# Seven copied row pairs in six buffers, gathers that wait for the rows in front, a written-out first pair and a deep block in the last pair, in an xDeepFM kernel on one NeuronCore

## The chip, the core and the metric

The kernel runs on one NeuronCore of a Trainium2 chip. The metric is device time in microseconds (us). The kernel before takes 447.75 us, the median of 3 runs (447.04 to 449.23).

## What is computed

The reference is one forward pass of xDeepFM over a batch of 512, with 26 features of a 32-wide embedding (`M`, `E`) and 13 dense inputs. Cut to its core:

```python
emb = tables[feat_idx, sparse]                       # (512, 26, 32)
linear_out = lin_sparse_w[feat_idx, sparse].sum(-1) + dense @ lin_dense_w
x0 = xk = emb
for w, bb in ((conv1_w, conv1_b), (conv2_w, conv2_b)):    # 128 outputs each
    hp = einsum('bhd,bmd->bhmd', xk, x0).reshape(-1, h * 26, 32)
    xn = sigmoid(einsum('oi,bid->bod', w, hp) + bb)
    xk = xn[:, :64]                                  # goes on to the next layer
    res.append(xn[:, 64:])                           # goes to the output
cin_out = concat(res).sum(-1) @ cin_w + cin_b
h1 = tanh(concat(emb, dense) @ W1 + b1)              # 845 -> 1024
h2 = tanh(h1 @ W2 + b2); h3 = tanh(h2 @ W3 + b3)     # 512, 256
return linear_out + cin_out + h3 @ deep_w + deep_b + bias
```

## The kernel before, in words

The 512 samples are worked through in 16 **pairs** (`NPAIR`), each of two chunks `c` of 16 samples; a chunk has 16 x 32 = 512 columns, so a tile of a pair has 1024. Five engines run programs of their own and meet through counters (semaphores).

**Rows in.** GpSimd's `gather(i)` fetches the embedding rows of pair `i` with 7 indirect DMAs (line 348). SyncE's queue writes them to HBM in another layout (`lay_out`, tensor `laid`), then reads them back in two forms: `fetch(i)` brings a raw tile of 26 rows (`raw`), and `copy(n)` brings a row pair broadcast to 128 partitions (`copied`, 2 DMAs of 256 KB). SyncE's queue also loads the deep weights (`load_piece`). It works strictly in order: per pair `NC` copies, a `lay_out` after the fourth, the `fetch` at the end. A copy into a buffer waits until TensorE has finished the tile that used it last (`main_done`).

**Layer 1.** ScalarE casts raw to `x` (`x_high`, line 524), VectorE computes the low part (`x_low`, line 629). TensorE forms sums of feature pairs (`sums_of`, line 396, three a pair), ScalarE squares them (`squares`), TensorE contracts the squares (`layer1`, line 412, two a pair), and ScalarE's `sigmoid` (line 544) gives `xk`.

**Layer 2.** It has 13 tiles `t` a pair (`T2`). For a tile, VectorE multiplies `xk` by rows of `x0` spread over the partitions (the product, line 696), and TensorE contracts the product (`main`, line 434). The spread rows come in one of two ways: for the tiles in `COPIED` from the buffers that DMA fills, for the tiles in `SPREAD` from PSUM, where TensorE puts them with a selection matmul (`spread_tile`, line 424). Sums and spreads share three PSUM slots (`ring`); an entry waits until the entry three places ahead of it in the list that `enter` makes has been read. Products of spread tiles go through three buffers (`prod`).

**The order** on TensorE is written out by tables: a pair has four groups (`GROUPS`), and `SUMS_IN`, `SPREADS_IN`, `L1_IN` say what stands in front of or behind the mains of each group. Before pair 0, TensorE runs `WARM` matmuls (line 447) whose result nothing uses.

**The deep part** comes last: ScalarE and GpSimd split the transposed embeddings into `xt_hi` and `xt_lo` (line 369), GpSimd splits ten weight pieces, and TensorE runs 8 + 4 + 2 blocks of `D1`, `D2`, `D3` outputs (line 491); a block of the first layer is 21 matmuls.

## Time and profile before

| | |
|---|---|
| median of 3 runs | 447.75 us |
| the profiled execution | 447.28 us, of which the span is 445.5 us |
| mean granted TensorE clock | 0.981 |
| TensorE busy | 423.0 us, 95% |
| VectorE busy | 318.5 us, 71% |
| ScalarE, GpSimd busy | 161.1 us, 164.2 us |
| DMA | 64.03 MB, mean 144 GB/s |
| chain that ended last | TensorE 74%, VectorE 11%, issue 11% |

Pair 0 begins when the first sums are formed and ends with its `main` of tile 12 at 69.24 us; pairs 1 to 14 follow without a visible seam up to 354.21 us, then pair 15 up to about 372 us, and the deep part up to 443.9 us. Busy shares are means over these stages. Ends of matmuls are modelled, so the distance between the starts of two rows tells more than the length of one. A row of the timeline with "x4" merges four records; an fp32 matmul leaves two records.

### The profile page before, as it was taken

Reading aid. Unit: us, or ns where it says so; the run is one execution under the profiler, and the core shown is the slowest. Engines: PE = TensorE matmul, PEld = TensorE weight load, DVE = VectorE, ACT = ScalarE, POOL = GpSimd, SP = SyncE. Lnnn points to the kernel's source line nnn. Section 1 sums busy time; section 2 is a strip of 40 time slices with the busy share of each in tenths; the row PEclk is TensorE's granted clock in tenths of the full one; section 3 lists DMA queues with packets and bytes.
Section 4 is the critical chain, followed back from the end, with each engine's and each line's share of the span. In section 5 each row is a group of like instructions: output and inputs, shape, how many; then the busy total and the mean of one; then the engine's idle time right before and its main releaser. Section 6 shows DMA issues by size and latency. Waiting matters only on the chain.

```text
span 445.5 us, 5390 instructions
## 1 busy us (share of the span) xinstructions
PE 423.0 (95%) x1961; PEld 176.5 (40%) x1961; DVE 318.5 (71%) x356; ACT 161.1 (36%) x264; POOL 164.2 (37%) x146
## 2 busy tenths in 40 slices
PE   3687989999999999999999999999999989999997
PEld 3662322333233332323333333323333225887784
DVE  3104568898989898988989898989889794522121
ACT  3027224444352634444453526344443321111011
POOL 6734516243343516172434436060000096840000
PEclk9978789999999999999999999999999999999999
DMA  5445477787878686877877686949657631310000
GB/s 189 91 113 119 100 181 168 186 198 171 184 187 194 171 205 162 192 181 175 196 176 190 179 195 157 227 125 211 183 148 162 146 94 47 97 48 1 0 0 0
DMA packets 38304, 64.03 MB, mean 144 GB/s; under 512 B 19601, under 2 KB 22033, under 8 KB 38278
## 3 DMA queue, kind: packets, MB, share of 16 engines
q1 hardware_dynamic: 34694, 61.93, 54.7%
q0 software_dynamic: 3584, 1.76, 4.2%
q8 instruction: 15, 0.25, 0.2%
q14 instruction: 11, 0.09, 0.1%
HBM read 61.96 MB, written 1.71 MB: 143 GB/s over the span
## 4 chain that ended last, share of the span: by engine, by line
PE 74%; DVE 11%; issue 11%; ACT 2%; SPq 1%; DVEq 0%; another core or an unknown queue 0%; DMA 0%; ACTq 0%
PE conv L434 32%; PE conv L412 18%; PE conv L491 7%; PE ring L491 7%; DVE copied L696 7%; PE ring L424 5%; PE ring L396 3%; DVE prod L696 3%; ACT sq L573 1%; ACT xk L544 0%; ACT sq L533 0%; DVEq L694 0%; PE conv L510 0%; PE conv L506 0%
## 5 line engine op out<-in xcount | busy, mean ns | idle before, releaser
L348 POOL DMA_INDIRECT emb<-in_table,rows x112 | 128.3, 1146 | 168.8 <-DMA laid<-emb 137.1
L696 DVE TENSOR_TENSOR prod<-ring,xk 128x1024 f32<-128x1024 f32 x112 | 133.8, 1218 | 38.0 <-PE ring L424 29.1
L696 DVE TENSOR_TENSOR copied<-copied,xk 128x1024 f32<-128x1024 f32 x96 | 114.2, 1230 | 0.4
L434 PE MATMUL conv<-prod,w_sb 128*64 128x512 f32 x448 | 114.4, 614 | 0.1
L434 PE MATMUL conv<-copied,w_sb 128*64 128x512 f32 x384 | 96.3, 603 | 2.9 <-DVE copied L696 2.0
L412 PE MATMUL conv<-sq,w_sb 117*64 117x512 f32 x384 | 90.4, 606 | 0.3 <-issue 0.3
L544 ACT ACTIVATE xk<-conv,const_sb 64x512 f32<-64x512 f32 x64 | 43.7, 682 | 126.3 <-PE conv L412 113.1
L533 ACT ACTIVATE sq<-ring 117x512 f32<-117x512 f32 x90 | 48.5, 595 | 31.5 <-PE ring L396 19.5
L434 PEld LDWEIGHTS conv<-copied,w_sb 128*64 128x64 f32 x384 | 24.7, 137 | 67.3 <-issue 38.3
L412 PEld LDWEIGHTS conv<-sq,w_sb 117*64 117x64 f32 x384 | 27.8, 139 | 55.9 <-issue 55.7
L434 PEld LDWEIGHTS conv<-prod,w_sb 128*64 128x64 f32 x448 | 26.7, 137 | 51.3 <-issue 43.4
L629 DVE TENSOR_TENSOR x<-raw,x 26x512 fp32r<-26x512 f32 x32 | 21.8, 683 | 27.7 <-issue 16.0
L424 PE MATMUL ring<-x,sel_sb 58*128 58x512 f32 x224 | 40.1, 418 | 0.4 <-DVE prod L696 0.2
L369 POOL TENSOR_TENSOR xt_lo<-xt,xt_hi 128x512 fp32r<-128x512 f32 (+1 forms) x7 | 14.2, 2061 | 56.4 <-ACT xt_hi L605 56.4
L424 PEld LDWEIGHTS ring<-x,sel_sb 58*128 58x128 f32 x224 | 20.0, 187 | 21.4 <-issue 17.2
L396 PE MATMUL ring<-x,sel_sb 58*117 58x512 f32 x96 | 23.9, 485 | 4.4 <-DVE prod L696 2.4
L724 DVE CAST h_hi<-hf 128x512 fp32r<-128x512 f32 x8 | 6.5, 819 | 26.6 <-ACT hf L617 26.6
L396 PEld LDWEIGHTS ring<-x,sel_sb 58*117 58x117 f32 x96 | 8.7, 173 | 40.6 <-issue 35.1
L546 ACT ACTIVATE res<-conv,const_sb 64x512 f32<-64x512 f32 x32 | 21.9, 684 | 0.8
L447 PE MATMUL conv<-sel_sb 128*117 128x234 f32 x113 | 17.2, 315 | 4.9 <-issue 4.9
L524 ACT ACTIVATE x<-raw 96x512 fp32r<-96x512 f32 x16 | 10.1, 631 | 27.2 <-DMA raw<-laid 25.8
L447 PEld LDWEIGHTS conv<-sel_sb 128*117 128x117 f32 x113 | 16.1, 223 | 6.2 <-issue 6.1
(76 smaller groups left out, 292.2 us busy)
## 6 DMA issues: line engine op xcount, KB each, us to landing
copied<-laid SPq DMA_DIRECT2D x192, 256.0 KB
wpiece<-in_mlp SPq DMA_DIRECT2D x22, 256.0 KB
emb<-in_table,rows POOLq DMA_INDIRECT x112
raw<-laid SPq DMA_DIRECT2D x32, 52.0 KB
laid<-emb SPq DMA_DIRECT2D x16, 96.0 KB, 2.9
sel_f<-in_sel SPq DMA_DIRECT2D x1, 832.0 KB, 5.6
const_sb<-in_const SPq DMA_DIRECT2D x1, 626.0 KB, 4.1
w_sb<-in_w SPq DMA_DIRECT2D x1, 416.0 KB, 6.2
```

The costliest lines, as they stand in the source:

```text
L348: pool.indirect_dma_start(out=emb[0:n, i, j, :], out_offset=None, in_=table, in_offset=bass.IndirectOffsetOnAxis(ap=rows[0:n, i, j:j + 1], ...
L396: mm = nc.tensor.matmul(sums_bank(i, u)[0:UK, c, :], sel1_sb[at:at + XK, u, :], x[i % RX][at:at + XK, :], start=True, stop=True)
L412: mm = nc.tensor.matmul(l1_bank(i, c)[o, :], w1_sb[:, u, o], sq[i % 2][0:UK, u, c, :], start=(u == 0), stop=(u == UT - 1))
L424: mm = nc.tensor.matmul(spread_bank(r)[:, c, :], sel2_sb[at:at + XK, t, :], x[i % RX][at:at + XK, :], start=True, stop=True)
L434: mm = nc.tensor.matmul(conv[i % 2][c * HALF:(c + 1) * HALF, :], w2_sb[:, t, :], prod_of(r)[:, c, :], start=(t == 0), stop=(t == T2 - 1))
L447: nc.tensor.matmul(conv[1][0:UK, 0:2 * UK], sel1_sb[:, 0, :], sel1_sb[:, 0:2, :].rearrange("p u k -> p (u k)"), start=True, stop=True)
L491: mm = nc.tensor.matmul(MLP_BANKS[n % 2], w[0:r, k, mt * P:(mt + 1) * P], h[0:r, k, :], start=(k == 0 and j == 0), stop=(k == kt - 1 and j ...
L533: nc.scalar.activation(sq[i % 2][0:UK, u, c, :], sums_bank(i, u)[0:UK, c, :], ACT.Square)\
L544: nc.scalar.activation(xk[i % 2][q * HALF:(q + 1) * HALF, c, :], bank[0:HALF, :], ACT.Sigmoid, bias=small_sb[0:HALF, C_CB1:C_CB1 + 1]).the ...
L546: nc.scalar.activation(res1[i % 2][c * HALF:(c + 1) * HALF, :], bank[HALF:P, :], ACT.Sigmoid, bias=small_sb[HALF:P, C_CB1:C_CB1 + 1]).then ...
L629: nc.vector.tensor_tensor(x[i % RX][at + XLO:at + XK, :], raw[i % RX][at:at + M, :], x[i % RX][at:at + M, :].bitcast(F32), ALU.subtract).t ...
L696: nc.vector.tensor_tensor(prod_of(r)[:, :, :].rearrange("p c n -> p (c n)"), left[:, :, :].rearrange("p c n -> p (c n)"), xk[i % 2][:, :, ...
```

## The change

Seven tiles instead of six are copied, and six instead of seven spread; the copies go through six buffers (`RC`) instead of five. The spreads of tiles 0 and 1 of a pair stand in the pair before. `gather(i)` waits for the rows of pair `i-1` to land, no longer for their rewritten form in `laid`; pair 1 waited for nothing before and now waits for the rows of pair 0. TensorE's order for pair 0 is written out, with all work of pair 0 and the matmuls for pair 1 in its own sequence. The 113 small warm matmuls become 13 fp32 matmuls of 512 columns on another tensor, which wait for `sel_in`. ScalarE casts `x` of pair 1 after the second sigmoid of pair 0, and VectorE computes the low part of pair 1 after tile 1. The first block of the deep part's first layer is issued in the last pair after tile 7, and waits for the `xt_lo` pieces one by one. Scratch tensors are merged (`lin_row` over `xt`, `clamped` into `wrap`).

```diff
@@ -38,19 +38,18 @@
 GSEM = 4
 RING = 3
 RP = 3
-COPIED = (1, 2, 3, 6, 7, 10)
+COPIED = (2, 3, 5, 6, 7, 10, 11)
 SPREAD = tuple(t for t in range(T2) if t not in COPIED)
 NC, NS = len(COPIED), len(SPREAD)
-RC = 5
+RC = 6
 LAY_AT = 3
+DEEP_AT = 1
 GROUPS = ((0, 1, 2, 3), (4, 5, 6, 7), (8, 9, 10, 11), (12,))
-SPREADS_IN = (((0, 4), (0, 5)), ((0, 8), (0, 9)), ((0, 11), (0, 12)), ((1, 0),))
-SUMS_IN = ({0: ((1, 0), (1, 1), (1, 2)), 2: ((2, 0),), 3: ((2, 1),)},
-           {0: ((1, 2),), 2: ((2, 0),), 3: ((2, 1),)})
-L1_AHEAD = ({0: 0}, {})
-L1_IN = ({0: 1}, {0: 0, 1: 1})
+SPREADS_IN = (((0, 4),), ((0, 8), (0, 9)), ((0, 12), (1, 0)), ((1, 1),))
+SUMS_IN = {0: ((1, 2),), 2: ((2, 0),), 3: ((2, 1),)}
+L1_IN = {0: 0, 1: 1}
 X_LOW_AT, TURN_AT, FOLD1_AT, PIECE_AT = (10, 5), 9, (5, 7), 11
-WARM = 113
+WARM = 13
 
 C_B1, C_B2, C_B3, C_DEEP, C_CB1, C_CB2, C_CIN1, C_CIN2, C_AUX, C_END = 0, 8, 12, 14, 16, 17, 18, 20, 22, 23
 SMALL_AT = 0
...
@@ -240,8 +239,16 @@
 
         for u in range(UT):
             enter(("sums", 0, u))
-        enter(("spread", 0))
-        for i in range(NPAIR):
+        enter(("spread", SPREAD[0]))
+        enter(("spread", SPREAD[1]))
+        for u in range(UT):
+            enter(("sums", 1, u))
+        for r in SPREAD[2:]:
+            enter(("spread", r))
+        for k in range(2):
+            enter(("sums", 2, k))
+            enter(("spread", T2 + SPREAD[k]))
+        for i in range(1, NPAIR):
             for g in range(len(GROUPS)):
                 for j, u in sums_in(i, g):
...
@@ -341,8 +348,8 @@
 
                 if i >= GSEM:
                     pool.wait_ge(rows_in[i % GSEM], ROWS * (i // GSEM))
-                if i >= 2:
-                    pool.wait_ge(laid_in[(i - 1) % RX], LAID * ((i - 1) // RX + 1))
+                if i:
+                    pool.wait_ge(rows_in[(i - 1) % GSEM], ROWS * ((i - 1) // GSEM + 1))
                 for j in range(GJ):
                     n = P if j < NG else ML * PB
                     pool.indirect_dma_start(
@@ -416,7 +423,7 @@
             def spread_tile(r):
 
                 i, t = r // T2, r % T2
-                if t == 0:
+                if t == SPREAD[0]:
                     pe.wait_ge(x_lo_done, 2 * (i + 1))
                 slot_free("spread", r)
...
@@ -435,6 +442,28 @@
                                           start=(t == 0), stop=(t == T2 - 1))
                 mm.then_inc(main_done, 1)
 
+            deep_layers = ((m1_hi, m1_lo, K1, xt_hi, xt_lo), (m2_hi, m2_lo, K2, h1_hi, h1_lo),
+                           (m3_hi, m3_lo, K3, h2_hi, h2_lo))
+
+            def deep(layer, mt):
+
+                hi, lo, kt, xh, xl = deep_layers[layer]
+                start = sum(MT[:layer])
+                n = start + mt
+                if n >= 2:
+                    pe.wait_ge(tanh_done, n - 1)
+                for k in range(kt):
+                    if n == 0:
+                        pe.wait_ge(xt_lo_done, k + 1)
+                    if layer and mt == 0:
+                        pe.wait_ge(h_lo_done, start - kt + k + 1)
+                    r = K1_LAST if layer == 0 and k == K1 - 1 else P
+                    for j, (w, h) in enumerate(((hi, xh), (lo, xh), (hi, xl))):
+                        mm = nc.tensor.matmul(MLP_BANKS[n % 2], w[0:r, k, mt * P:(mt + 1) * P],
+                                              h[0:r, k, :], start=(k == 0 and j == 0),
+                                              stop=(k == kt - 1 and j == 2))
+                mm.then_inc(mlp_done, 1)
+
             pe.wait_ge(const_in, 16)
             pe.wait_ge(w1_step, 2)
             for u in range(UT):
@@ -442,57 +471,63 @@
                                       start=(u == 0), stop=(u == UT - 1))
             mm.then_inc(fix_done, 1)
 
+            pe.wait_ge(sel_in, 16)
+            for k in range(WARM):
+                nc.tensor.matmul(conv[1][:, :], sel2_f[:, 0, :], sel2_f[:, 0:4, :].rearrange("p t o -> p (t o)"),
+                                 start=True, stop=True)
             pe.wait_ge(sel_done, 1)
-            for k in range(WARM):
-                nc.tensor.matmul(conv[1][0:UK, 0:2 * UK], sel1_sb[:, 0, :], sel1_sb[:, 0:2, :].rearrange("p u k -> p (u k)"),
-                                 start=True, stop=True)
             for u in range(UT):
                 sums_of(0, u)
             pe.wait_ge(w1_step, 4)
             layer1(0, 0)
             pe.wait_ge(sel_done, 2)
-            spread_tile(0)
+            spread_tile(SPREAD[0])
+            spread_tile(SPREAD[1])
             layer1(0, 1)
             pe.wait_ge(w2_in, 16)
-            for i in range(NPAIR):
+            for u in range(UT):
+                sums_of(1, u)
+                main(u)
+            spread_tile(SPREAD[2])
+            main(3)
+            spread_tile(SPREAD[3])
+            layer1(1, 0)
+            for r in SPREAD[4:-1]:
+                spread_tile(r)
+            for t in range(4, 8):
+                main(t)
+            spread_tile(SPREAD[-1])
+            layer1(1, 1)
+            for t in range(8, T2 - 1):
+                main(t)
+            for k in range(2):
+                sums_of(2, k)
+                spread_tile(T2 + SPREAD[k])
+            main(T2 - 1)
+            for i in range(1, NPAIR):
                 for g, tiles_now in enumerate(GROUPS):
                     for j, u in sums_in(i, g):
                         sums_of(j, u)
                     for r in spreads_in(i, g):
                         spread_tile(r)
-                    if g in L1_AHEAD[min(i, 1)]:
-                        layer1(i + 1, L1_AHEAD[min(i, 1)][g])
                     for t in tiles_now:
                         main(T2 * i + t)
-                    if g in L1_IN[min(i, 1)] and i + 1 < NPAIR:
-                        layer1(i + 1, L1_IN[min(i, 1)][g])
+                    if i == NPAIR - 1 and g == DEEP_AT:
+                        pe.wait_ge(piece_lo, KW)
+                        pe.wait_ge(l2_read, NPAIR - 1)
+                        deep(0, 0)
+                    if g in L1_IN and i + 1 < NPAIR:
+                        layer1(i + 1, L1_IN[g])
 
             pe.wait_ge(lin_step, 1)
             nc.tensor.matmul(ring[1][0:NPAIR, 1, 0:PB], lin[:, :], ind_sb[:, :], start=True, stop=False)
             nc.tensor.matmul(ring[1][0:NPAIR, 1, 0:PB], emb[0:ML * PB, :, NG, E], ind_sb[0:ML * PB, :],
                              start=False, stop=True).then_inc(lin_done, 1)
 
-            pe.wait_ge(xt_lo_done, K1)
-            pe.wait_ge(l2_read, NPAIR - 1)
-            n = 0
-            for layer, (hi, lo, kt, xh, xl) in enumerate((
-                    (m1_hi, m1_lo, K1, xt_hi, xt_lo), (m2_hi, m2_lo, K2, h1_hi, h1_lo),
-                    (m3_hi, m3_lo, K3, h2_hi, h2_lo))):
-                before = sum(MT[:layer])
+            for layer in range(3):
                 pe.wait_ge(piece_lo, (KW, KW + K2, PIECES)[layer])
-                for mt in range(MT[layer]):
-                    if n >= 2:
-                        pe.wait_ge(tanh_done, n - 1)
-                    for k in range(kt):
-                        if layer and mt == 0:
-                            pe.wait_ge(h_lo_done, before - kt + k + 1)
-                        r = K1_LAST if layer == 0 and k == K1 - 1 else P
-                        for j, (w, h) in enumerate(((hi, xh), (lo, xh), (hi, xl))):
-                            mm = nc.tensor.matmul(MLP_BANKS[n % 2], w[0:r, k, mt * P:(mt + 1) * P],
-                                                  h[0:r, k, :], start=(k == 0 and j == 0),
-                                                  stop=(k == kt - 1 and j == 2))
-                    mm.then_inc(mlp_done, 1)
-                    n += 1
+                for mt in range(1 if layer == 0 else 0, MT[layer]):
+                    deep(layer, mt)
                 if layer == 0:
 
                     pe.wait_ge(fold1_done, NPAIR)
@@ -573,8 +608,8 @@
                     nc.scalar.activation(sq[0][0:UK, u, c, :], sums_bank(0, u)[0:UK, c, :], ACT.Square).then_inc(sq_done, 1)
             act.wait_ge(sel_done, 2)
             sigmoid(0, 0)
+            sigmoid(0, 1)
             x_high(1)
-            sigmoid(0, 1)
             for u in range(UT):
                 squares(1, u)
             sigmoid(1, 0)
...
@@ -677,7 +712,6 @@
             dve.wait_ge(w1_step, 3)
             nc.vector.tensor_copy(w1_sb[:, :, :], w1a_sb[:, :, :]).then_inc(w1_step, 1)
             x_low(0)
-            x_low(1)
 
             for i in range(NPAIR):
                 for t in range(T2):
@@ -698,6 +732,8 @@
                                             xk[i % 2][:, :, :].rearrange("p c n -> p (c n)"),
                                             ALU.mult).then_inc(prod_done, 1)
                     k = min(i, 1)
+                    if i == 0 and t == 1:
+                        x_low(1)
                     if t == X_LOW_AT[k] and i + 2 < NPAIR:
                         x_low(i + 2)
                     if t == FOLD1_AT[k]:
```

**TensorE at the start.** First before, then after: from the warm matmuls on (`sel_sb`, `sel_f`) into pair 0; `sq` is read by `layer1`, `x` by sums (117 rows) and spreads (128 rows).

```order
L447 MATMUL conv<-sel_sb 117x234 x113
L396 MATMUL ring<-x_81,sel_sb 117x512 x6
L412 MATMUL conv<-sq_64,w_sb 64x512 x6
L424 MATMUL ring<-x_81,sel_sb 128x512 x2
L412 MATMUL conv<-sq_64,w_sb 64x512 x6
L396 MATMUL ring<-x_82,sel_sb 117x512 x6
L424 MATMUL ring<-x_81,sel_sb 128x512 x4
L412 MATMUL conv<-sq_65,w_sb 64x512 x6
L434 MATMUL conv<-prod_70,w_sb 64x512 x2
```

```order
L476 MATMUL conv<-sel_f 128x512 x13
L403 MATMUL ring<-x_81,sel_sb 117x512 x6
L419 MATMUL conv<-sq_63,w_sb 64x512 x6
L431 MATMUL ring<-x_81,sel_sb 128x512 x4
L419 MATMUL conv<-sq_63,w_sb 64x512 x6
L403 MATMUL ring<-x_82,sel_sb 117x512 x2
L441 MATMUL conv<-prod_69,w_sb 64x512 x2
L403 MATMUL ring<-x_82,sel_sb 117x512 x2
L441 MATMUL conv<-prod_70,w_sb 64x512 x2
```

The sums of pair 1 now alternate with the first mains of pair 0, and layer 1 of pair 1 stands behind them.

**TensorE where one pair passes into the next.** First before, then after: from the sums ahead of tile 12 to the first mains of the next pair (`prod` and `copied` name the two kinds of product).

```order
L396 MATMUL ring<-x_81,sel_sb 117x512 x2
L424 MATMUL ring<-x_83,sel_sb 128x512 x2
L434 MATMUL conv<-prod_71,w_sb 64x512 x2
L396 MATMUL ring<-x_81,sel_sb 117x512 x2
L424 MATMUL ring<-x_83,sel_sb 128x512 x4
L434 MATMUL conv<-prod_72,w_sb 64x512 x2
L434 MATMUL conv<-copied_75,w_sb 64x512 x2
```

```order
L403 MATMUL ring<-x_81,sel_sb 117x512 x2
L431 MATMUL ring<-x_83,sel_sb 128x512 x2
L441 MATMUL conv<-prod_71,w_sb 64x512 x2
L403 MATMUL ring<-x_81,sel_sb 117x512 x2
L431 MATMUL ring<-x_83,sel_sb 128x512 x2
L441 MATMUL conv<-prod_69,w_sb 64x512 x2
L441 MATMUL conv<-prod_70,w_sb 64x512 x2
L441 MATMUL conv<-copied_74,w_sb 64x512 x2
```

The spread behind the first sums was that of the next pair's tile 0 and is now that of its tile 1; behind the second sums stands one spread (tile 4) instead of two.

**TensorE in the last pair.** After the change, behind tile 7 (before, the spread of the next group followed at once): 21 matmuls of the deep part, of which the first three and the last three are shown, then the spread of tile 12.

```order
L441 MATMUL conv<-copied_72,w_sb 64x512 x2
L441 MATMUL conv<-copied_73,w_sb 64x512 x2
L462 MATMUL conv<-xt_hi,m_hi 128x512
L462 MATMUL conv<-xt_hi,m_lo 128x512
L462 MATMUL conv<-xt_lo,m_hi 128x512
...
L462 MATMUL conv<-xt_hi,m_hi 128x512
L462 MATMUL conv<-xt_hi,m_lo 128x512
L462 MATMUL conv<-xt_lo,m_hi 128x512
L431 MATMUL ring<-x_81,sel_sb 128x512 x2
L441 MATMUL conv<-prod_69,w_sb 64x512 x2
L441 MATMUL conv<-prod_70,w_sb 64x512 x2
```

The block moved from behind the last pair to its middle; tiles 8 to 12 stand behind it.

## Rows read from the trace of the kernel before

**Rows 1.** Page, part 1: busy time, share of the span, instructions, by engine.
```profile
PE 423.0 (95%) x1961; PEld 176.5 (40%) x1961; DVE 318.5 (71%) x356; ACT 161.1 (36%) x264; POOL 164.2 (37%) x146
```

**Rows 2.** Stretches: length, busy PE, PEld, DVE, ACT, POOL (x count), clock, DMA, GB/s.
```profile
42.05:69.24 27.19, 25.74 (x96) 8.00 (x96) 17.05 (x18) 9.36 (x17) 12.18 (x11) 0.81 0.54 133
69.24:354.21 284.97, 284.17 (x1342) 89.99 (x1340) 257.73 (x279) 124.36 (x205) 95.04 (x81) 1.00 0.75 180
354.21:372.10 17.89, 15.49 (x66) 3.72 (x64) 17.07 (x18) 4.44 (x8) 14.17 (x7) 1.00 0.26 75
...
301.00:322.00 21.00, 20.94 (x102) 6.73 (x101) 19.10 (x22) 9.62 (x16) 0.00 (x0) 1.00 0.79 195
...
89.62:110.00 20.38, 20.32 (x98) 6.44 (x96) 18.50 (x21) 9.06 (x15) 7.72 (x8) 1.00 0.77 183
...
62.30:66.00 3.70, 3.70 (x11) 1.17 (x12) 2.32 (x2) 0.72 (x2) 0.96 (x2) 0.55 0.67 163
```

**Rows 3.** Timeline, TensorE, one pair: start us, us, line, operation, idle before.
```profile
77.32 1.94 PE L434 MATMUL conv<-prod,w_sb 128*64 128x512 f32 x8
...
80.81 2.75 PE L412 MATMUL conv<-sq,w_sb 117*64 117x512 f32 x12
...
88.28 0.40 PE L424 MATMUL ring<-x,sel_sb 58*128 58x512 f32 x2
88.61 1.08 PE L434 MATMUL conv<-prod,w_sb 128*64 128x512 f32 x4
...
89.95 0.63 PE L424 MATMUL ring<-x,sel_sb 58*128 58x512 f32 x4
90.51 1.08 PE L434 MATMUL conv<-prod,w_sb 128*64 128x512 f32 x4
...
94.43 2.75 PE L412 MATMUL conv<-sq,w_sb 117*64 117x512 f32 x12
```

**Rows 4.** Timeline, VectorE: first product of a pair.
```profile
88.78 1.23 DVE L696 TENSOR_TENSOR prod<-ring,xk 128x1024 f32<-128x1024 f32 x1 [1.58 <-PE conv L434]
```

**Rows 5.** Timeline, TensorE, the start.
```profile
8.52 9.60 PE L447 MATMUL conv<-sel_sb 128*117 128x234 f32 x72
...
30.55 0.95 PE L396 MATMUL ring<-x,sel_sb 58*117 58x512 f32 x6
...
34.99 2.80 PE L412 MATMUL conv<-sq,w_sb 117*64 117x512 f32 x12
```

**Rows 6.** Timeline, all engines, the start.
```profile
12.72 0.91 POOL L348 DMA_INDIRECT emb<-in_table,rows  x1 [0.30 <-issue]
...
14.94 0.38 SPq L274 DMA_DIRECT2D laid<-emb  x1
...
20.08 1.40 DVE L629 TENSOR_TENSOR x<-raw,x 26x512 fp32r<-26x512 f32 x2 [10.72 <-ACT x L524]
...
28.85 0.72 SPq L287 DMA_DIRECT2D raw<-laid  x2
...
31.08 3.05 ACT L573 ACTIVATE sq<-ring 117x512 f32<-117x512 f32 x6 [11.04 <-issue]
...
39.35 1.39 ACT L544 ACTIVATE xk<-conv,const_sb 64x512 f32<-64x512 f32 x2 [1.88 <-remote]
```

**Rows 7.** Stretches of 1 us, TensorE alone: busy, matmul records, granted clock.
```profile
9.50:10.50 1.00, 1.00 (x7) 1.00 0.05 9
12.50:13.50 1.00, 1.00 (x12) 1.00 0.22 17
```

**Rows 8.** Timeline, ScalarE: the cast of a landed raw tile.
```profile
93.45 0.63 ACT L524 ACTIVATE x<-raw 96x512 fp32r<-96x512 f32 x1 [2.05 <-DMA raw<-laid]
```

**Rows 9.** Timeline, GpSimd, last pair.
```profile
355.76 14.17 POOL L369 TENSOR_TENSOR xt_lo<-xt,xt_hi 128x512 fp32r<-128x512 f32 x7 [56.40 <-ACT xt_hi L605]
```

**Rows 10.** Line 696 in the last pair: count, ns min/median/max, first and last start.
```profile
L696 DVE TENSOR_TENSOR copied<-copied,xk x6: 1172/1252/2305, 354.9 to 367.4; 128x1024 f32<-128x1024 f32 x6
```

**Rows 11.** Chain that ended last: start us, us, what.
```profile
377.53 4.78 PE ring L491 x21
```

More of the change, by code:

```diff
@@ L97, in build @@
         lin16 = sb("lin16", [NPAIR, PB])
-        lin_row = sb("lin_row", [1, B])
         row_sb = sb("row_sb", [1, B])
@@ L125, in build @@
         emb = sb("emb", [P, NPAIR, GJ, ROW])
+        at_xt = space(0)
         xt = sb("xt", [P, K1, B])
+        lin_row = sb("lin_row", [1, B], F32, at_xt)
         idx_sb = sb("idx_sb", [P, 2, NPAIR, GJ], I32)
@@ L129, in build @@
         inside = sb("inside", [P, NPAIR, GJ])
-        clamped = sb("clamped", [P, NPAIR, GJ])
         rows = sb("rows", [P, NPAIR, GJ], U32)
@@ L201, in sums_in @@
         def sums_in(i, g):
-            return [(i + ahead, u) for ahead, u in SUMS_IN[min(i, 1)].get(g, ()) if i + ahead < NPAIR]
+            return [(i + ahead, u) for ahead, u in SUMS_IN.get(g, ()) if i + ahead < NPAIR]
         def spreads_in(i, g):
@@ L662, in _ @@
             dve.wait_ge(idx_step, 2)
-            nc.vector.tensor_scalar(clamped[:, :, :], inside[:, :, :], 0.0, float(V - 1), ALU.max, ALU.min)\
+            nc.vector.tensor_scalar(wrap[:, :, :], inside[:, :, :], 0.0, float(V - 1), ALU.max, ALU.min)\
               .then_inc(idx_step, 1)
             dve.wait_ge(idx_step, 3)
-            nc.vector.tensor_tensor(rows[:, :, :], clamped[:, :, :], idx_sb[:, 1, :, :], ALU.add).then_inc(idx_step, 2)
+            nc.vector.tensor_tensor(rows[:, :, :], wrap[:, :, :], idx_sb[:, 1, :, :], ALU.add).then_inc(idx_step, 2)
             nc.vector.memset(aux[:, :], 1.0).then_inc(zeroed, 1)
```

## The prediction, made before the changed kernel ran

> **What bounds the kernel now.** I read the page's busy line first, then the stretches, the timelines of one pair, the start and the last pair, and the row of the copied product. The busy line has TensorE at 95% of the span and VectorE at 71% [rows 1]. The stretches show where the mean comes from: from 69.24 to 354.21 us TensorE is busy 284.17 of 284.97 us at a granted clock of 1.00, so pairs 1 to 14 take 284.97/14 = 20.36 us each [rows 2]. The reader is to see that this is not quite pure work. In one pair, four mains that wait for nothing take 80.81 - 77.32 = 3.49 us, 0.87 each, while the first four of a pair take 94.43 - 90.51 = 3.92 us [rows 3]: they come right behind VectorE, which sat idle 1.58 us before its first product [rows 4], until TensorE had put that tile's rows down ahead of tile 12. VectorE is busy 18.50 us of a period of 20.38 [rows 2], so TensorE is the bound and VectorE close behind. The start is different: the warm matmuls begin at 8.52 us and the sums stand behind them until 30.55 [rows 5], though VectorE had finished the low part of pair 0 at 20.08 + 1.40 = 21.48 [rows 6]. And pair 15 has VectorE as its bound: 17.07 us busy of 17.89 [rows 2].
>
> **The warm matmuls.** A full-width fp32 matmul of 512 columns is in no row. The nearest is a main, two half-width ones side by side: 0.87 us. Thirteen cost 11.3 us. The array begins slow: in the stretch of 1 us at 9.5 there are 7 matmul records and at 12.5 there are 12 [rows 7], nearly twice as many, while the clock column says 1.00 in both; so the first 3 us run at half rate, which adds 1.5. They begin where the old ones did and end at 8.5 + 11.3 + 1.5 = 21.3, just when the low part is there. Bounds: half rate throughout, 22.6 us, ending at 31.1; 0.44 us each if only half of a main's time is needed, ending near 15.7, with TensorE idle until 21.5. I take 21.5 for the first sums, against 30.55.
>
> **Pair 0.** From the first sums to the end of the second layer-1 block it took 34.99 + 2.80 - 30.55 = 7.24 us [rows 5]; one more spread costs 0.33 (88.61 - 88.28) [rows 3], so 29.1. The second sigmoid follows at once, since the cast of pair 1 no longer stands ahead of it: xk is whole at 29.1 + 0.1 + 1.39 = 30.6. It was 40.74, and 1.88 of that was a wait on something unknown (an instruction that came late, I think) [rows 6].
> Next is the low part of pair 1, for which the written-out order waits before the first main. Its gathers now wait for the rows of pair 0, which landed at 14.94; they began at 12.72 [rows 6], so all behind them is 2.2 us later: the fetch goes from 28.85 to 31.1. What follows the fetch lies between its issue of 0.72 us and the whole 20.08 - 14.94 = 5.1 us that pair 0 needed from landed rows to low part; I take 2.3, so the low part starts at 33.4 (31.8 to 36.2) and its first half is there at 34.1. The products of tiles 0 and 1 are done by then. From there TensorE has 13 mains (11.3), two layer-1 blocks (2.7 each, 5.4), five sums and six spreads (11 x 0.3 = 3.3) and some 0.4 of change-over: 20.4 us. It stood idle from 29.1 to 34.1, and before the change such idle was followed by half clock: the stretch 42.05:69.24 has a mean clock of 0.81, which is 27.19 x 0.19 = 5.2 us lost, of which 62.30:66.00 at 0.55 is 1.7 [rows 2] and an earlier fall the other 3.5. I take 3.0 (0 to 3.5). The spread of pair 1's tile 1 uses the slot of the sums of pair 2 put down two entries before, and so waits for ScalarE's squares: 0.65. With 0.35 for a late instruction like the one above, pair 0 ends at 34.1 + 20.4 + 3.0 + 0.65 + 0.35 = 58.5 instead of 69.24: **-10.7 us** (-6 to -14.5). Copies 6 and up wait for mains of pair 0 as before, and gain the lead of the sixth buffer.
>
> **Pairs 1 to 14.** TensorE loses one spread a pair, the second of two: two take 90.51 - 89.95 = 0.56, one 0.33 [rows 3], so 0.23. The spread of tile 0 stands a group earlier, so VectorE need not stand idle 1.58 us before it, runs ahead, and the first four mains fall from 3.92 towards 3.49; I take 0.37 of the 0.43. What is late next: the sums at a pair's start now wait for product 0 of the same pair, which VectorE forms right behind product 12. VectorE's work is unchanged, 13 products whether copied or spread; in a period of 20.36 - 0.60 = 19.76 us its 18.50 leave 1.26. So 14 x 0.60 = **-8.4 us**. Bounds: 14 x 0.66 = -9.2 and, if VectorE gets stuck, 0 or worse.
> The DMA cost of the seventh copy: 2 DMAs of 256 KB. The best stretch, 195 GB/s at a share of 0.79 [rows 2], is 247 GB/s at a full share, so 512 KB take 2.1 us on top of 0.77 x 20.38 = 15.7: 17.8 of 19.76, a share of 0.90. The gathers crowd into the first half of the run; their own share is small, as 0.77 with them (89.62:110) and 0.79 without (301:322) shows. Each copied buffer is reissued nine or more tiles ahead of its product, some 13 us, against a queue of two copies, 4.2 us, so I cost the copies at nothing. The fetch is what hangs on the queue: it stands behind one more main (0.87) and one more copy (2.1), and ScalarE already waits 2.05 us for the raw tile [rows 8]. It lands 0 to 3.0 us later; the low part stands in VectorE's line behind product 5, and behind it all later products. VectorE's 1.26 us cover most of this; that is the rival A below. The gathers' new wait holds up nothing but gathers, since GpSimd has no other work until the last pair.
>
> **The last pair.** The moved block saves 4.78 us behind the pair [rows 11]. But in its new place it waits for xt_lo: those seven pieces start 1.55 us after the pair and take 14.17 us [rows 9], so the last is there at 15.7, and with its three matmuls TensorE leaves the block at 16.4 + 0.2. Tiles 8 to 12 are queued behind it: a spread 0.33, four mains 3.5, the last 1.0, end at 21.4 instead of 17.9. That is 3.5 paid for 4.78, -1.3. In the block TensorE works 0.7 of every 2.0 us, for some 5 us; I take it that the clock falls as in 62.30:66.00, for 1.8. Together **+0.5 us** (-1.3 to +3.5).
>
> **Sum.** -10.7 - 8.4 + 0.5 = -18.6 on the profiled execution's 447.28 us (span 445.5 and 1.8 around it) gives 428.7. The median of the runs is 0.47 higher, so 429.2; I say 429. Its own range is 425 to 434.
>
> **A rule weighed.** Copied products in the last pair, beside GpSimd's subtractions, took up to 2305 ns, where the shortest took 1172 [rows 10]: one was blocked for 1.1 us. Beside gathers nothing of the kind shows: VectorE is busy 18.50 of 20.38 us with them and 19.10 of 21.00 without, 91% both [rows 2]. The Trainium skill, page "SBUF — State Buffer", section "Who interferes with whom", says that a VectorE instruction with two inputs in SBUF blocks against a GpSimd instruction that reads SBUF; a copied product has two such inputs, a spread one has one. By that rule a gather, which reads its row numbers, could block too, and the trace so far bears it out only for the subtractions.
>
> **Rivals.**
> *A, the raw tile late.* The fetch's 3.0 us exceed VectorE's 1.26, products fall behind, and a pair takes about 20.4 again. For it: ScalarE's wait of 2.05 and a DMA share of 0.90. Against: VectorE is ahead by the 1.58 us that it no longer sits idle. All of the 8.4 is lost: 437.5. Chance 0.13.
> *B, the clock holds* in pair 0 and in the last pair: 429 - 3.0 - 1.8 = 424. For it: the last pair before had 2.4 us of idle at clock 1.00 [rows 2]. Against: the two falls above. Chance 0.12.
> *C, the warm matmuls stay long,* 22.6 us: the start gains nothing of its 9.1 us, 438.5. Rows 7 speak against it. Chance 0.04.
> *D, slower: the DMA queues do not carry it.* No long stretch shows a share above 0.79. If that is a ceiling, a pair needs 17.8/0.79 = 22.5 us, 14 x 2.2 = 30 more, less 10.2: 468. It decides from a period of 20.36 + 10.2/14 = 21.1, a ceiling of 0.84. Against it: the DMA is idle between bursts, for want of issues. Chance 0.05.
> *E, gathers block copied products:* 7 x 1.1 = 7.7 us a pair less 1.3, over the 9 pairs beside gathers, 58 us: 487. Chance 0.02.
> The forecast keeps 0.64. Below 423 and above 438 lie about two in ten. A measurement of this kernel tells 0.5%, 2.2 us, from no change; forecast, A, B and C all lie beyond that on the fast side, 0.93, and D and E on the slow side, 0.07; I give 0.01 of each to the middle: faster 0.92, within 0.5% 0.02, slower 0.06.
>
> **What would show it.** First sums at 21.5 (start right) or near 31 (C). The last main of pair 0 near 58.5, with half clock around 34 to 41; no dip is B. A period near 19.8 with VectorE idle 1.3 us; idle before the low part of x, and 20.4, is A; a DMA share flat at its ceiling and waits for copies is D; copied products above 2 us beside gathers is E. In the last pair TensorE should wait about 2 us between the triples of the deep block, and leave tile 12 some 21 to 23 us after the pair began. I am wrong if TensorE has gaps in pairs 2 to 14, or if pair 0 ends after 63.

## The result, and the profile after

The changed kernel takes 434.53 us, the median of 5 runs (433.08 to 436.81), against 447.75 for the kernel before (444.98 to 449.23, 5 runs): a ratio of 0.972, 95% interval 0.968 to 0.976. Forecast were 429.0 us and a range of 423 to 438. The profiled execution took 434.31 us, with a span of 431.8; the span before was 445.5.

The page's busy line, which answers to [rows 1]:

```profile
PE 410.6 (95%) x1842; PEld 164.2 (38%) x1842; DVE 320.9 (74%) x356; ACT 160.4 (37%) x264; POOL 171.5 (40%) x146
```

TensorE worked 12.4 us less, the span fell by 13.7. Where that lies is told by the stretches, one a pair, from the sums ahead of tile 12 on, and the rest (columns as in [rows 2]):

```profile
59.57:82.48 22.91, 20.20 (x96) 6.26 (x94) 18.35 (x21) 8.96 (x15) 13.28 (x11) 1.00 0.95 226
82.48:102.31 19.83, 19.83 (x98) 6.35 (x96) 18.38 (x21) 9.08 (x15) 12.98 (x10) 1.00 0.94 216
102.31:122.87 20.56, 20.20 (x96) 6.26 (x94) 18.43 (x21) 8.96 (x15) 10.28 (x9) 1.00 0.88 211
122.87:142.63 19.76, 19.76 (x96) 6.44 (x94) 18.41 (x21) 9.08 (x15) 13.43 (x10) 1.00 0.88 216
...
202.57:223.27 20.70, 20.22 (x96) 6.26 (x94) 18.36 (x21) 8.96 (x15) 12.80 (x10) 1.00 0.94 213
223.27:243.75 20.48, 20.28 (x97) 6.28 (x96) 18.42 (x21) 8.97 (x15) 7.12 (x8) 1.00 0.92 210
243.75:263.51 19.76, 19.76 (x97) 6.45 (x96) 18.42 (x21) 9.08 (x15) 0.00 (x0) 1.00 0.85 210
...
342.14:363.21 21.07, 18.87 (x83) 7.74 (x81) 17.79 (x15) 4.32 (x8) 13.84 (x7) 1.00 0.34 88
363.21:431.80 68.59, 66.27 (x287) 51.11 (x285) 19.79 (x26) 10.28 (x16) 20.41 (x20) 1.00 0.11 31
```

Pair 0 ends at 59.57 instead of 69.24 (-9.67). Pairs 1 to 14 take 342.14 - 59.57 = 282.57 us instead of 284.97 [rows 2] (-2.4). The last pair takes 21.07 instead of 17.89 (+3.18), and what is behind it 68.59 instead of 445.5 - 372.1 = 73.4 (-4.8). Together -13.7. The reader is to see that eight of the fourteen pairs run at 19.83 us or less, TensorE busy all the time (pair 14, behind which no further pair's sums are formed, takes 19.31). The other six (1, 3, 6, 7, 8, 9) take 22.91, 20.56, 20.20, 19.96, 20.70 and 20.48, and all of them lie while gathers still run: the last gather is issued at 236.4 us.

What stands in the way in pair 1: first ScalarE, then VectorE, TensorE and SyncE's queue, each from its own timeline (start, length, what, and in brackets the idle time before and what ended it):

```profile
68.26 0.63 ACT L559 ACTIVATE x<-raw 96x512 fp32r<-96x512 f32 x1 [6.91 <-DMA raw<-laid]
```
```profile
68.92 1.40 DVE L664 TENSOR_TENSOR x<-raw,x 26x512 fp32r<-26x512 f32 x2 [4.49 <-ACT x L559]
70.35 1.23 DVE L730 TENSOR_TENSOR copied<-copied,xk 128x1024 f32<-128x1024 f32 x1
```
```profile
71.63 2.21 PE L441 MATMUL conv<-copied,w_sb 128*64 128x512 f32 x8 [2.65 <-DVE copied L730]
```
```profile
56.93 0.39 SPq L281 DMA_DIRECT2D laid<-emb  x1
57.37 0.55 SPq L283 DMA_DIRECT2D laid<-emb  x1
58.02 3.74 SPq L305 DMA_DIRECT2D copied<-laid  x6
61.85 0.91 SPq L294 DMA_DIRECT2D raw<-laid  x2
```

TensorE's idle time was ended by a product, but VectorE had sat idle 4.49 us for the cast, and ScalarE 6.91 for the raw tile. The fetch was issued at 61.85, behind six DMAs of copies of 256 KB each, and landed only before 68.26. The waits over the whole run (us, times, longest):

```profile
ACT x L559 <- DMA raw<-laid: 61.1, 14, 10.2
DVE x L664 <- ACT x L559: 25.9, 10, 10.8
```

Before, ScalarE's waits for raw tiles summed to 25.8 us in 13 ([rows 8] is one of them), and VectorE had a single wait for the cast, at the start [rows 6].

### The profile page after: what moved, and what is told of

Its sections match the earlier page's. It is cut to its first block and busy times, and to the rows that moved or that the text cites. A ratio compares the mean times of both kernels' runs of the same rounds, so it can differ in the third digit from the quotient of the medians.

```text
span 431.8 us, 5184 instructions
## 1 busy us (share of the span) xinstructions
PE 410.6 (95%) x1842; PEld 164.2 (38%) x1842; DVE 320.9 (74%) x356; ACT 160.4 (37%) x264; POOL 171.5 (40%) x146
## 5 line engine op out<-in xcount | busy, mean ns | idle before, releaser
L355 POOL DMA_INDIRECT emb<-in_table,rows x112 | 135.6, 1211 | 99.5 <-DMA emb<-in_table,rows 68.1
L730 DVE TENSOR_TENSOR copied<-copied,xk 128x1024 f32<-128x1024 f32 x112 | 135.7, 1247 | 0.5
L730 DVE TENSOR_TENSOR prod<-ring,xk 128x1024 f32<-128x1024 f32 x96 | 114.1, 1216 | 23.1 <-PE ring L431 13.1
L441 PE MATMUL conv<-copied,w_sb 128*64 128x512 f32 x448 | 107.0, 595 | 5.5 <-DVE copied L730 5.1
L441 PE MATMUL conv<-prod,w_sb 128*64 128x512 f32 x384 | 98.4, 619 | 0.0
L441 PEld LDWEIGHTS conv<-copied,w_sb 128*64 128x64 f32 x448 | 30.9, 137 | 72.3 <-issue 50.2
L441 PEld LDWEIGHTS conv<-prod,w_sb 128*64 128x64 f32 x384 | 22.1, 137 | 41.2 <-issue 36.9
L431 PE MATMUL ring<-x,sel_sb 58*128 58x512 f32 x192 | 35.7, 419 | 0.9 <-ACT sq L568 0.9
L559 ACT ACTIVATE x<-raw 96x512 fp32r<-96x512 f32 x16 | 10.1, 629 | 61.1 <-DMA raw<-laid 61.1
L431 PEld LDWEIGHTS ring<-x,sel_sb 58*128 58x128 f32 x192 | 16.8, 185 | 21.2 <-issue 15.8
L589 ACT ACTIVATE res<-conv,const_sb 128x512 f32<-128x512 f32 x16 | 11.0, 689 | 22.9 <-PE conv L441 22.9
```

The source lines that it names most:

```text
L355: pool.indirect_dma_start(out=emb[0:n, i, j, :], out_offset=None, in_=table, in_offset=bass.IndirectOffsetOnAxis(ap=rows[0:n, i, j:j + 1], ...
L431: mm = nc.tensor.matmul(spread_bank(r)[:, c, :], sel2_sb[at:at + XK, t, :], x[i % RX][at:at + XK, :], start=True, stop=True)
L441: mm = nc.tensor.matmul(conv[i % 2][c * HALF:(c + 1) * HALF, :], w2_sb[:, t, :], prod_of(r)[:, c, :], start=(t == 0), stop=(t == T2 - 1))
L730: nc.vector.tensor_tensor(prod_of(r)[:, :, :].rearrange("p c n -> p (c n)"), left[:, :, :].rearrange("p c n -> p (c n)"), xk[i % 2][:, :, ...
```

## The experiments

Ratios are to the kernel before, run beside them on the same chip: 447.06 us beside 1 to 4, 447.37 beside 5 to 8, 439.73 beside 9 to 11. So the last three are compared with one another. Across groups a ratio carries some 1.3%: one and the same program has 0.959 in experiment 2 and 0.972 in 11, since the kernel before was 7 us faster beside 11 (why is open), the program itself 1.2 us. The changed kernel (434.53 us, 0.972) ran beside none of the three groups; what an edit does to it is told by the traces, pair by pair.

**1. Gathers without the new wait.** The changed kernel with

```diff
-                if i:
-                    pool.wait_ge(rows_in[(i - 1) % GSEM], ROWS * ((i - 1) // GSEM + 1))
```

> The changed kernel, but a gather waits no longer for the rows of the pair in front (only for its own counter's last use). In the changed kernel the rows of pair 3 landed at 56.9 us, SyncE's queue stood at their rewriting until then, the raw tile of pair 3 was cast at 68.26 us and pair 1 took 22.9 us. Theory G (the gathers' pace is what pair 1 waits for): gathers follow each other at about 9 us instead of 13 to 17, rows of pair 3 land by 46 us, pair 1 takes 20.0 us or less, the rest is as it was or pays up to 1 us more in pairs 2 to 6, where gathers now crowd; about 2 to 3 us faster than the changed kernel, span 429 to 430. Theory C (the seventh copy fills the DMA queues and that alone makes the raw tile late): pair 1 stays above 22 us, since more DMA work comes earlier; span 432 or more.

Measured: 546.56 us (546.37 to 547.79), ratio 1.225 (1.221 to 1.229). Neither theory had such a loss. All 112 gathers follow one another every 1.25 us until about 144 us. The stretch 50:140, then its DMA queues, then TensorE's timeline, then ScalarE's:

```profile
50.00:140.00 90.00, 13.08 (x34) 3.20 (x34) 6.12 (x6) 6.89 (x11) 68.03 (x73) 0.55 0.13 13
```
```profile
DMA packets 2305, 1.15 MB, mean 13 GB/s; under 512 B 1152, under 2 KB 2304, under 8 KB 2304
q0 software_dynamic: 2304, 1.14, 13.1%
q8 instruction: 1, 0.02, 0.1%
```
```profile
115.60 1.40 PE L401 MATMUL ring<-x,sel_sb 58*117 58x512 f32 x2 [74.66 <-DVE x L662]
```
```profile
66.19 1.39 ACT L577 ACTIVATE xk<-conv,const_sb 64x512 f32<-64x512 f32 x2 [31.01 <-issue]
110.93 1.39 ACT L577 ACTIVATE xk<-conv,const_sb 64x512 f32<-64x512 f32 x2 [42.64 <-issue]
```

In 90 us the DMA engines are 87% idle, no byte of SyncE's queue moves, and one packet of instructions comes through. ScalarE (last fence) stands 31 and 42.6 us with no wait that the profile shows. The silence of SyncE's queue is in part a consequence: its next copy needs TensorE's product of tile 2, which is done at 122.9 us, but it is issued only at 158.53, 35.6 us after that. So a wait that was costed at nothing is worth 112 us: what it gives is a pause in the gathers.

**2. The fetch ahead of the sixth copy** instead of behind the seventh:

```diff
+FETCH_AT = 5
                 for k in range(NC):
                     n = NC * i + RC + k
+                    if k == FETCH_AT and i + RX < NPAIR:
+                        fetch(i + RX)
...
-                if i + RX < NPAIR:
-                    fetch(i + RX)
```

> The changed kernel, but the fetch of a raw tile stands before the sixth of the seven copies of a pair in SyncE's queue instead of behind the seventh. Theory Q (the raw tile is late because it queues behind two copies, 4.2 us of DMA): ScalarE's wait for the raw tile falls from 61 us in all to under 30, VectorE's wait before the low part goes in pairs 3 and 6 to 9, which took 20.2 to 20.7 us and now take 19.8; pair 1 gains 2 of its 3.1; span about 427. Theory G (pair 1 waits for the gathers and the others for PSUM or for copies): pair 1 stays near 22.9, and the others keep their 0.4 to 0.9; span 431 to 432.

Measured: 428.13 us (427.16 to 428.33), ratio 0.959 (0.956 to 0.962), 1.5% less than the changed kernel's 434.53. SyncE's queue, ScalarE's cast, and the stretches from pair 2 on:

```profile
58.54 1.18 SPq L306 DMA_DIRECT2D copied<-laid  x2
59.82 0.91 SPq L295 DMA_DIRECT2D raw<-laid  x2
60.83 2.37 SPq L306 DMA_DIRECT2D copied<-laid  x4
```
```profile
64.25 0.63 ACT L560 ACTIVATE x<-raw 96x512 fp32r<-96x512 f32 x1 [2.56 <-DMA raw<-laid]
```
```profile
79.66:99.43 19.77, 19.77 (x96) 6.43 (x94) 18.41 (x21) 9.09 (x15) 10.38 (x9) 1.00 0.97 223
99.43:218.07 118.64, 118.64 (x566) 38.61 (x564) 110.58 (x121) 54.57 (x90) 62.18 (x50) 1.00 0.94 217
218.07:316.94 98.87, 98.87 (x472) 32.17 (x471) 92.08 (x101) 44.98 (x75) 26.45 (x18) 1.00 0.90 215
```

The fetch goes 2.0 us earlier, the cast 4.0. Pair 1 takes 19.76 and pairs 2 to 13 take 19.77; TensorE is busy without a gap, at a DMA share of 0.97 and 0.94. Pairs 1 to 14 take 276.36 us together instead of 282.57: moving the fetch takes the whole loss away. That it is the only way to do so is not shown; see 3 and 5. The last pair is 21.07, as without the edit.

**3. Six copied tiles, six buffers.** `COPIED = (2, 3, 6, 7, 10, 11)`, tile 5 spread beside tile 4 again, the fetch late.

> The changed kernel with tile 5 spread instead of copied: six copied tiles in six buffers, seven spreads, all else as changed. If the seventh copy costs more in DMA queueing than its spread saves: DMA share near 0.80 in pairs 1 to 9 instead of 0.88 to 0.95, no wait before the low part from pair 2 on, every pair 20.0 us (19.77 and one more spread at 0.23), 14 pairs 280 to 281 against 282.6; span 429 to 431. If the seventh copy pays: every pair at 20.3 as before, since the spreads again meet full PSUM slots, 14 pairs 284 to 285; span 434.

Measured: 431.61 us (428.64 to 432.43), ratio 0.966 (0.963 to 0.970). Every pair from 1 to 13 takes 20.01 us (one 20.29), beside gathers or not: together 260.37 us, against 263.26 in the changed kernel. So the seventh copy saves 20.01 - 19.77 = 0.24 a pair, the 0.23 that one spread was costed at, and the new order and buffers alone bring 20.38 - 20.01 = 0.37, just what was taken for the order. In the traces the seventh copy's time in the queue, behind which the fetch stands, cost 6.0 and saved 3.1, net 2.9 us. By the times alone, the intervals just overlap.

**4. Both 1 and 2.**

> The changed kernel with both: a gather waits for no rows in front, and the fetch stands before the sixth copy. Theories G and Q together: every pair from 1 to 13 at 19.8 us, 14 pairs 276.5 instead of 282.6, span 425.5 to 426.5. If either fails, as much of the 6.1 us stays as its own run shows.

Measured: 546.57 us (545.95 to 549.05), ratio 1.226 (1.222 to 1.229), as in 1. An early fetch doesn't help while the engines stand still.

**5. The old wait for the gathers**, in the changed kernel:

```diff
-                if i:
-                    pool.wait_ge(rows_in[(i - 1) % GSEM], ROWS * ((i - 1) // GSEM + 1))
+                if i >= 2:
+                    pool.wait_ge(laid_in[(i - 1) % RX], LAID * ((i - 1) // RX + 1))
```

> The changed kernel with the gathers' old wait: from pair 2 on a gather waits for the rewritten rows of the pair in front, pair 1 for nothing. Theory P (the new wait brings almost nothing, gathers are early enough either way after pair 3): the gathers go back to one set a pair, rows of pair 3 land at 57 to 59 us instead of 56.9, pair 1 stays at 22.5 to 24, pairs 6 to 9 lose less to crowding, span 430 to 434. Theory W (the new wait was needed for the shorter pairs): the rows come late again in pairs 2 to 5, span 436 or more.

Measured: 432.26 us (432.13 to 436.78), ratio 0.969 (0.963 to 0.975), not told apart from the changed kernel's. Pair 1 takes 23.42 in its trace, pairs 2 to 13 take 19.76 to 19.87, with TensorE busy throughout:

```profile
83.96:321.53 237.57, 237.57 (x1130) 76.81 (x1128) 220.72 (x241) 109.06 (x180) 96.52 (x76) 1.00 0.89 214
```

The same twelve pairs take 240.35 us in the changed kernel. So with the fetch as late as there, but gathers paced by `laid` (pauses of 8.2 to 11.3 us from pair 5 on, the last gather at 289.2 us), pairs 3 and 6 to 9 lose nearly nothing. By these traces, one each, their lateness needs three things at once: the late fetch (2), the seventh copy (3), and gathers as dense as the new wait lets them be (5); without any one of them it is gone. For pair 1 the old wait is no remedy. The sum of ScalarE's waits is no measure of the loss: it is 60.1 us here and 61.1 in the changed kernel. By the times, with the late fetch, either wait will do.

**6. Two pairs of gathers in flight**: the wait is for the rows of pair `i - 2`.

> The changed kernel, a gather waits for the rows of two pairs in front instead of one, so two sets may be under way. Without any such wait all engines stood still for some 100 us while gathers were issued without a pause, with one instruction packet moved from 50 to 140 us. Theory I (gathers issued without a pause hold back the engines' instruction loading): the first 14 gathers run on without a pause from 4.3 to 22 us as in the kernel before, TensorE and ScalarE show idle time with no releaser between 18 and 45 us, pair 0 ends 2 to 10 us later than 59.57, and later pairs show such gaps too; span 434 to 450. Theory N (only an unlimited run of gathers does harm): no such gaps, pair 1 at 20.5 or less since rows come earlier, span 428 to 430.

Measured: 547.03 us (544.12 to 547.89), ratio 1.220 (1.214 to 1.225). The wait never bites, for the rows of the pair before last have landed by then, and gathers follow every 1.25 us as in 1. Both theories missed. A bound that never bites does not help; in every run that did well GpSimd stopped after each seven gathers. Whether it is the stop itself or the smaller number in flight that counts was not separated.

**7. The deep block behind the last pair**, all eight together:

```diff
-                    if i == NPAIR - 1 and g == DEEP_AT:
-                        pe.wait_ge(piece_lo, KW)
-                        pe.wait_ge(l2_read, NPAIR - 1)
-                        deep(0, 0)
```

> The changed kernel with all eight blocks of the deep part's first layer behind the last pair, as before. The moved block was worth 4.8 - 3.2 = 1.6 us by the two traces (last pair 21.07 instead of 17.89 us). So: last pair 17.9 to 18.3, deep part 4.8 longer, span 433.4 instead of 431.8. If the last pair stays near 21 without the block, its length came from copied products blocked by GpSimd, and the span is 436.6.

Measured: 438.15 us (434.87 to 438.52), ratio 0.976 (0.971 to 0.981). Last pair 18.5 us, the rest 73.3, together 91.8 against 21.07 + 68.59 = 89.66: moving the block gains 2.2 us. So the first branch of the expectation holds for the last pair, though the span of 436.7 is that of the second: pairs 1 to 14, whose code is untouched, take 286.23 us against 282.57, with 25.34, 21.16, 20.76 and 21.33 for the slow ones, and pair 0 ends 0.9 earlier. So the raw tile's lateness scatters from one kernel to the next by some microseconds.

**8. The kernel before with the new warm matmuls only.**

> The kernel before with the 13 new warm matmuls and nothing else. First sums at 21.8 instead of 30.55. Pair 0's tables are the old ones: layer 1 of pair 1 stands ahead of the first main, ScalarE casts pair 1 between the sigmoids. If the warm matmuls alone make the start: pair 0 ends near 60, as in the changed kernel, span 436. If the written-out order is needed too: the first product starts at 33 to 34 instead of 30.8, pair 0 ends at 62 to 65, pairs 1 to 15 as before, span 438.5 to 441.5.

Measured: 442.45 us (442.23 to 444.15), ratio 0.990 (0.986 to 0.994). First sums at 22.06, pair 0 ends at 64.08. The warm matmuls alone bring 5.2 of pair 0's 9.7 us; the written-out order and the rest, not taken apart, bring the other 4.5.

**9. Experiment 2, and the clock held.** Five unused matmuls in TensorE's idle time, ahead of the sums of pair 1:

```diff
+            for k in range(HOLD):
+                nc.tensor.matmul(conv[0][0:HALF, :], w2_sb[:, 0, :], w2_sb[:, 0:8, :].rearrange("p t o -> p (t o)"),
+                                 start=True, stop=True)
```

> The changed kernel with the early fetch, and five matmuls on the layer-2 weights that nothing uses, in TensorE's idle time ahead of the first sums of pair 1 (29 to 34 us). Theory H (the half clock from 34 to 40 us follows from that idle time): the clock stays at 1.00, the first sums and two mains take 4.4 us instead of 7, pair 0 ends near 57.3 instead of 59.9, span 423.3. Theory D (pair 0 is bound by rows and products whatever the clock): pair 0 ends at 59.5 or later, as the rows of pair 3 land at 57.4 and the mains wait; span 425.9 or more. In between: pair 0 is 2.6 shorter, but pair 1 gives it back, since the raw tile of pair 3 lands when it did; span 425.9, too.

Measured: 427.94 us (426.22 to 431.16), ratio 0.974 (0.971 to 0.976). TensorE alone in stretches of 4 us (length, busy, records, granted clock, DMA share, GB/s), the changed kernel first:

```profile
30.00:34.00 4.00, 0.02 (x1) 0.88 1.03 242
34.00:38.00 4.00, 4.00 (x10) 0.50 1.05 221
38.00:42.00 4.00, 4.00 (x14) 0.76 0.41 86
```
```profile
30.00:34.00 4.00, 3.63 (x9) 1.00 0.99 219
34.00:38.00 4.00, 3.81 (x16) 1.00 1.04 221
38.00:42.00 4.00, 4.00 (x18) 1.00 0.49 108
```

The clock stays at its full 2.4 GHz and pair 0 ends at 57.25, 2.65 us earlier than in 2. But the rows of pair 3 land no sooner: they are laid out at 57.46 (57.45 in 2), the fetch is issued at 59.82 in both, and pair 1, which needs it, takes 24.40 instead of 19.76. The raw tile itself came later, too: it is cast at 65.72 instead of 64.25. TensorE then stood idle 2.44 us, and behind that the clock fell:

```profile
70.00:74.00 4.00, 3.94 (x12) 0.58 1.06 227
```

Over pair 1 the mean clock is 0.93, 1.7 us lost; with the idle time that is most of the 4.6. In this execution the gain is more than given back. It was the longest of the six (431.16); the others took 426.2 to 429.1, so how much is kept as a rule stays open, but the median tells no difference from 11.

**10. Experiment 2 with the old wait for the gathers.**

> The changed kernel with the early fetch and the gathers' old wait (for the rewritten rows of the pair in front, from pair 2 on). Theory Q (the place of the fetch in the queue was all that was late): every pair from 1 on at 19.8 us as with the early fetch alone, span 425.5 to 427. Theory P (the gathers' pace matters once the fetch is early, above all for pair 1): pair 1 at 20.5 or more and a span above 427.

Measured: 434.87 us (433.31 to 436.0), ratio 0.990 (0.987 to 0.992). Pair 1 takes 19.76, but later periods reach 22.19 us, and ScalarE waits 63.2 us for raw tiles. SyncE's queue at pair 4, here and in 2:

```profile
80.15 0.39 SPq L282 DMA_DIRECT2D laid<-emb  x1
```
```profile
75.52 0.39 SPq L282 DMA_DIRECT2D laid<-emb  x1
```

Gathers that wait for `laid` start later (pair 4's at 61.21 instead of 58.20, pair 5's at 83.15 instead of 76.26), their rows land later, and the lay-out, which the early fetch needs at once, is 4.6 us late. The new wait earns its place only together with the early fetch.

**11. Experiment 2 again**, beside 9 and 10.

> The changed kernel with the early fetch once more, beside the two others on the same chip: median 427 to 428.5, every pair from 1 on at 19.77 us. If its pairs scatter as those of the changed kernel did (19.8 to 22.9 us), the early fetch was lucky the first time and has not removed the cause.

Measured: 426.94 us (426.56 to 428.83), ratio 0.972 (0.970 to 0.975), pairs 1 to 13 at 19.77 again. Against 9 (0.974) no difference can be told; against 10 (0.990) it is 1.8%. In microseconds these are the fastest versions that ran, 426.56 to 428.83 here and 427.16 to 428.33 in 2 against 433.08 to 436.81 for the changed kernel, which never ran beside them; the ratio of 0.972 is no better than the changed kernel's, and that 6 to 7 us are gained rests on these times and on the 6.2 us in pairs 1 to 14 of both traces.

## Why the prediction was right, point by point

The sign and the range held; the point was 5.5 us too low. That the time lies inside the range is no merit of the middle term, of which less than a third came. Of the three terms the first was off by 1.0 us, the last by 2.1 and the middle one by 6.0.

**The start.** Predicted: first sums at 21.5, idle until 34.1, end at 58.5. TensorE's timeline, which answers to [rows 5]:

```profile
8.46 13.46 PE L476 MATMUL conv<-sel_f 128*128 128x512 f32 x26
21.84 0.96 PE L403 MATMUL ring<-x,sel_sb 58*117 58x512 f32 x6
...
33.98 1.39 PE L403 MATMUL ring<-x,sel_sb 58*117 58x512 f32 x2 [4.68 <-issue]
```

They came at 21.84, 33.98 and 59.57. The price of 0.87 us for a full-width fp32 matmul, taken from two half-width ones side by side, nearly held: 13 took 13.46 us with the slow beginning, where 12.8 was worked out. Rival C is out. The clock fell to half behind the idle time, as taken: by the two stretches in experiment 9 it cost 4 x 0.50 + 4 x 0.24 = 2.96 us (3.0 taken), and holding it gained 2.65. Rival B falls for pair 0. The squares' stall was 0.71 (0.65 taken). The missing 1.1 us lies in the work between 33.98 and 59.57 and was not taken apart further.

That TensorE's idle time ended at 34 us was luck in part, for the path was another. I read the gather at 12.72 [rows 6] as the first of pair 1; it is the seventh of pair 0, and pair 1's began at 13.93. In the changed kernel they begin at 15.12, 1.2 us later and not 2.2, the rows land no later (the lay-out goes at 25.57, before at 25.73), and the fetch goes at 27.81, not at 31.1. SyncE's queue and VectorE:

```profile
27.81 0.72 SPq L294 DMA_DIRECT2D raw<-laid  x2
```
```profile
30.77 2.36 DVE L730 TENSOR_TENSOR prod<-ring,xk 128x1024 f32<-128x1024 f32 x2 [9.33 <-ACT xk L579]
33.16 1.40 DVE L664 TENSOR_TENSOR x<-raw,x 26x512 fp32r<-26x512 f32 x2
```

ScalarE cast the raw tile at 31.47 without waiting for it. The low part started at 33.16 because it stands behind VectorE's products of tiles 0 and 1, which began with the second sigmoid's end: 30.74 us, where 30.6 was worked out. Both ways give 33 us; the one that decided was not the rows.

**The step that failed: pairs 1 to 14, -8.4 us, measured -2.4.** The working of a pair was right: 19.76 us predicted, 19.77 undisturbed, in the clean pairs of the changed kernel and in pairs 1 to 13 of experiments 2 and 11. In experiment 2, where nothing is late, the fourteen pairs take 8.6 us less than before. What failed was the step "VectorE's 1.26 us cover most of this". I had the lateness at 0 to 3.0 us and gave the case that it is not covered, rival A, 0.13. It held in six pairs of fourteen: 6.2 us were lost there, 3.14 of them in pair 1, which starts with the new lead of pair 0 but with rows that land no earlier. Counted from the pair's start, ScalarE's cast stood at 2.4 to 3.8 us before; now it stands at 4.8 to 5.7 in the clean pairs and in pair 7, 5.4 in pair 6, 6.2 to 6.5 in pairs 3, 8 and 9, and 8.7 in pair 1. So the lateness was 2 to 3 us and more, the upper end of what I took, and nearly 6 in pair 1; what VectorE covered was, by the clean pairs, about 2 us and not 1.26. Experiment 2 takes away only the fetch's place and brings all of it back; 3 shows that the seventh copy is needed for the loss as well, and 5 the same of the dense gathers, but for pair 1. The dense gathers come from the new wait, which I had costed at nothing. Rival A's price, all of the 8.4, was too high, since it meant every pair: behind 243.75, where no gathers run, no pair is late.

**The DMA's share** was predicted at 0.90 and is 0.85 to 0.95 beside gathers, 0.75 to 0.85 without. Rival D falls: with the early fetch 0.97 and 0.94 are carried with no gap on TensorE. "I am wrong if TensorE has gaps in pairs 2 to 14" did come true: TensorE is idle 0.16 to 0.48 us in pairs 3, 6, 8 and 9, and these pairs and 7 are 0.2 to 0.9 us longer than the clean ones.

**"The gathers' new wait holds up nothing but gathers"** was true and missed the point: experiments 1 and 6 show that pauses in the gathers carry the rest of the kernel.

**The last pair, +0.5, measured +3.18 - 4.8 = -1.6.** Length predicted 21.4, measured 21.07. TensorE in the last pair:

```profile
349.30 1.08 PE L441 MATMUL conv<-copied,w_sb 128*64 128x512 f32 x4 [0.54 <-DVE copied L730]
351.54 1.08 PE L441 MATMUL conv<-copied,w_sb 128*64 128x512 f32 x4 [1.16 <-DVE copied L730]
352.54 0.50 PE L462 MATMUL conv<-xt_hi,m_hi 128*128 128x512 f32 x1
...
357.44 0.50 PE L462 MATMUL conv<-xt_hi,m_hi 77*128 77x512 f32 x1 [0.50 <-POOL xt_lo L376]
```
```profile
345.79 5.69 DVE L730 TENSOR_TENSOR copied<-copied,xk 128x1024 f32<-128x1024 f32 x3
```
```profile
343.55 13.84 POOL L376 TENSOR_TENSOR xt_lo<-xt,xt_hi 128x512 fp32r<-128x512 f32 x7 [106.25 <-ACT xt_hi L640]
```

GpSimd's pieces took 13.84 us (14.17 taken, [rows 9]). But the block began only at 352.54, 10.4 us into the pair, for TensorE waited 1.7 us in all for copied products, three of which (VectorE's row) took 5.69 us beside GpSimd, where three of 1.22 take 3.7. By then GpSimd had been at the pieces for 9 us, and all but the last were there when TensorE asked for them: the block waited once, 0.50 us, for the seventh. That last piece set the block's end, as predicted: it was there 15.25 us into the pair (15.7 taken), and the rest followed as worked out. Only where TensorE stood idle came out otherwise: I had it waiting for nearly every piece and the clock falling for 1.8; it stayed at 1.00. That 1.8 and the 0.33 of the length make the 2.1 us by which the sum of the two was better than forecast, and the last pair bears out this half of rival B. For the slow copied products the Trainium skill, "SBUF — State Buffer", section "Who interferes with whom", has the rule that a VectorE instruction with two inputs in SBUF contends with a GpSimd instruction that reads SBUF. The trace agrees here as in [rows 10]: 1.9 us each instead of 1.2. Beside gathers, from 59 to 244 us, the longest of 64 copied products took 1.225 us (count, ns min/median/max):

```profile
L730 DVE TENSOR_TENSOR copied<-copied,xk x64: 1206/1217/1225, 59.8 to 244.0; 128x1024 f32<-128x1024 f32 x64
```

So gathers block none, and rival E falls.

Sum of the misses against the profiled execution: +1.0 (pair 0), +6.0 (pairs 1 to 14) and -2.1 (the last pair and what is behind it) make 4.9, beside 0.7 in what lies around the span (2.5 us instead of 1.8): 5.6, from the 428.7 predicted for it to 434.3.

## What to carry to other kernels

A small transfer on which a chain of engines hangs shouldn't stand in a queue behind large ones that are needed much later: where a change adds a transfer, ask what is queued behind it, and what else will run at that time. A cover of 1.26 us is not to be set against a lateness of 0 to 3.0 us as though its mean were enough; each pair in which it doesn't suffice pays, and none gives anything back. And a wait that seems to hold up nothing may be what leaves room for others; take it out alone before you call it free.
